# Neighbour sum: compact weight blocks for half a batch, spread by DMA into a block-diagonal buffer

## What is computed

```python
idx = _knn(x_loc, k)                          # k = 30 neighbours of each of 1024 points
...
att = jax.nn.softmax(h[..., 0], axis=-1)      # one weight per point and neighbour
xk = x.transpose(0, 2, 1)[bidx, idx]
agg = jnp.einsum('bnkc,bnk->bnc', xk, att)    # the neighbour sum
return x + agg.transpose(0, 2, 1)
```

## Time and profile before

| | before |
|---|---|
| median of three runs | 8177.31 us |
| the profiled execution's own time | 8177.04 us |
| its span, first to last instruction | 8175.2 us |
| VectorE busy over the span | 7178.0 us (88%) |
| TensorE busy over the span | 5788.3 us (71%) |
| GpSimd busy over the span | 4651.6 us (57%) |
| ScalarE busy over the span | 4377.7 us (54%) |
| granted TensorE clock, mean | 0.801 of full speed |

### The profile page before, as it was taken

How to read it: one execution, slowest core, us unless ns; L and a number is a source line. 1 busy time by engine, 2 the same in 40 slices (tenths; PEclk the granted TensorE clock), 3 DMA queues, 4 the chain that set the end, 5 groups by cost and what they waited for, 6 DMA issues and landing times. The chain is left out here.

```text
span 8175.2 us, 225464 instructions
## 1 busy us (share of the span) xinstructions
PE 5788.3 (71%) x83468; PEld 3497.5 (43%) x83468; DVE 7178.0 (88%) x9524; ACT 4377.7 (54%) x16920; POOL 4651.6 (57%) x4269
## 2 busy tenths in 40 slices
PE   7888778878877888887778778787100177777777
PEld 3444444444444444444444444444000155555555
DVE  7998988888898888989888888998498798888898
ACT  6666666666666666666666666665222322222222
POOL 5677777777777777777777777776300122222222
PEclk8888888888888888888888888887555588788888
DMA  1211112221111222211121221112300011100000
GB/s 40 70 65 65 65 65 75 74 68 66 65 65 65 75 68 74 66 65 65 65 75 65 75 67 65 65 65 75 99 0 0 14 33 33 33 28 33 32 32 28
DMA packets 245175, 459.06 MB, mean 56 GB/s; under 512 B 152636, under 2 KB 178492, under 8 KB 211260
## 3 DMA queue, kind: packets, MB, share of 16 engines
q1 hardware_dynamic: 244028, 443.74, 16.2%
HBM read 378.65 MB, written 65.01 MB: 54 GB/s over the span
## 5 line engine op out<-in xcount | busy, mean ns | idle before, releaser
L641 ACT ACTIVATE prob<-SC,row_max 128x64 f32<-128x64 f32 x6144 | 1829.8, 324 | 1733.7 <-DVE row_max L956 1599.3
L745 POOL TENSOR_TENSOR k_bd<-k_t,head_mask 128x512 f32<-128x512 f32 x1536 | 1642.0, 1090 | 30.6 <-issue 20.0
L756 POOL TENSOR_TENSOR prob<-prob,row_rec 128x512 f32<-128x512 f32 x768 | 799.5, 1041 | 1356.9 <-DVE row_rec L964 1345.5
L932 DVE MAX8 top<-dist 128x8 f32<-128x1024 f32 x1024 | 1248.1, 1219 | 126.5 <-DVE dist L934 65.0
L641 ACT ACTIVATION_READ_ACCUMULATOR prob<-SC,row_max 128x1 f32 x6144 | 1331.8, 217 | 0.0
L936 DVE FIND_INDEX8 nbr<-top,dist 128x8 uint16<-128x1024 f32 x1024 | 1247.8, 1219 | 0.3 <-issue 0.3
L549 PE MATMUL PT<-ident,prob 128*128 128x128 f32 x3072 | 600.0, 328 | 689.3 <-ACT prob_t L648 685.8
L1493 PE MATMUL DM<-placed,d_oh_a 128*128 128x32 bf16 x24576 | 675.7, 181 | 432.3 <-DVE placed L1652 382.0
L541 PE MATMUL SC<-k_bd,q_t 128*64 128x256 f32 x6144 | 955.8, 438 | 0.0
L1534 ACT ACTIVATE sph_all<-DM 128x512 f32<-128x512 f32 x512 | 305.7, 597 | 1197.6 <-PE DM L1493 1197.6
L934 DVE MATCH_REPLACE8 dist<-top,dist 128x1024 f32<-128x1024 f32 x768 | 927.5, 1208 | 0.0
(11 more groups left out here) (191 smaller groups left out, 11234.4 us busy)
## 6 DMA issues: line engine op xcount, KB each, us to landing
low_all<-low_scratch SPq DMA_DIRECT2D x256, 1024.0 KB, 4.9
ctx<-in_ctx SPq DMA_DIRECT2D x32, 512.0 KB, 4.5
mask<-in_mask SPq DMA_DIRECT2D x32, 512.0 KB, 7.3
xb<-in_x SPq DMA_DIRECT2D x32, 512.0 KB, 3.7
x_scratch<-xb SPq DMA_DIRECT2D x32, 512.0 KB, 5.1
y_scratch<-y_b SPq DMA_DIRECT2D x32, 512.0 KB, 6.6
d_x<-x_scratch SPq DMA_DIRECT2D x32, 512.0 KB, 3.8
d_y<-y_scratch SPq DMA_DIRECT2D x32, 512.0 KB, 3.3
```

Of the source, the lines that this page charges most:

```text
L641: last = act.activation(prob[:, s % 4, g * CHUNK:(g + 1) * CHUNK], SC[:, s % 2, g * CHUNK:(g + 1) * CHUNK], ACT.Exp, bias=row_max[:, s % 2 ...
L745: last = pool.tensor_tensor(k_bd[:, q % 2, ch, :].rearrange("p (h k) -> p h k", h=8), kk, hm, ALU.mult)
L756: pool.tensor_tensor(pr, pr, row_rec[:, r % 2, :].unsqueeze(2).to_broadcast([128, 8, CHUNK]), ALU.mult).then_inc(normed, 1)
L932: last = dve.max(top8[:, k, :], dist[:, tt % 2, :])
```

## The change

The matrix that TensorE reads as moving operand is block-diagonal: a partition has non-zero weights in its own quarter's 8 columns alone. The new kernel computes these 8 columns only (`compact`), for four tiles at a time (`QG` = 128 columns of groups), and four DMAs per half batch, one for each quarter of 32 partitions, copy them into their own block of `placed`. `placed` now holds half a batch in each of two slots and is set to zero once at the start. The moving operand of a matmul is then read from `placed` with a step of `QG` elements. GpSimd's parts are no longer written twice. x2, y3, y and the transposed x2 move into free space of `sph_all`, and SyncE's order of loads and stores is rewritten around the new DMAs. Unchanged names stand as before.

```diff
+QG = NT // 2 * GROUPS
-        hj2 = sb("hj2", [128, BPD, NT, GROUPS, 2], BF16)
+        hi1 = sb("hi1", [128, 2, QG], BF16)
+        iota_m = sb("iota_m", [128, 8 * QG], BF16)
-        at3 = sb("at3", [128, BPD, 3, NT, GROUPS, 2], BF16)
+        at3 = sb("at3", [128, BPD, 3, 2, QG], BF16)
-        oh_j = sb("oh_j", [128, 2, GROUPS, 32], BF16)
-        placed = sb("placed", [128, 2, 3, GROUPS, 32], BF16)
-        x2 = sb("d_x2", [128, BPD, T])
-        y3 = sb("d_y3", [128, BPD, T])
-        x2_t = sb("x2_t", [128, BPD, NT, 128])
+        oh_m = sb("oh_m", [128, 2, 8, QG], BF16)
+        compact = sb("compact", [128, 2, 3, 8, QG], BF16)
+        placed = sb("placed", [128, 2, 4, 3, 8, QG], BF16)
+        spare = [keep["sph"][:, c, 8 * HALF:8 * HALF + 4 * T].rearrange("p (w u n) -> p w u n", w=2, u=BPD) for c in (0, 2)]
+        x2, y3 = spare[0][:, 0], spare[0][:, 1]
+        x2_t, y = spare[1][:, 0].rearrange("p u (t c) -> p u t c", t=NT), spare[1][:, 1]
...
+            def spread_blocks(i, u, h):
+                b = counter(i, u)
+                sp.wait_ge(compact_ready, START + b(2, h + 1))
+                if is_first(i, u):
+                    sp.wait_ge(cleared[h], START + 1)
+                else:
+                    sp.wait_ge(dense_ready, START + b(2 * NT, NT * (h - 1)))
+                for q in range(4):
+                    sp.dma_start(placed[32 * q:32 * q + 32, h, q, :, :, :], compact[32 * q:32 * q + 32, h, :, :, :]).then_inc(placed_in[h], 16)
             def body(i, u):
                 b = counter(i, u)
+                spread_blocks(i, u, 1)
+                if not is_first(i, u):
+                    before, slot = counter(i, u - 1), (u - 1) % BPD
+                    if not is_last(i, u):
+                        sp.wait_ge(xt_ready, START + before(1, 1))
+                        sp.wait_ge(xy_ready, START + before(1, 1))
+                        sp.dma_start(x2[:, slot, :], dram["x2"][b(1, 1)]).then_inc(x2_in[slot], 16)
+                        sp.wait_ge(read_out, START + before(2, 2))
+                        sp.dma_start(y3[:, slot, :], dram["y3"][b(1, 1)]).then_inc(y3_in[slot], 16)
+                    sp.wait_ge(normed, START + before(1, 1))
+                    sp.dma_start(dram["out"][before(1)], y[:, slot, :]).then_inc(out_done[slot], 16)
+                if not is_last(i, u):
+                    spread_blocks(i, u + 1, 0)
+            spread_blocks(0, 0, 0)
             all_batches(sp, body)
...
                     pe.wait_ge(oh_ready, START + b(NT, t + 1))
-                    pe.wait_ge(placed_ready, START + b(NT, t + 1))
+                    if t % 4 == 0:
+                        pe.wait_ge(placed_in[t // 4], START + b(64, 64))
...
-                                last = pe.matmul(DM[:, x % DM_BANKS, (g % 16) * 32:(g % 16 + 1) * 32], oh_a[:, t % 2, g, :],
-                                                 placed[:, t % 2, part, g, :], start=(part == 0), stop=(part == 2))
+                                last = pe.matmul(DM[:, x % DM_BANKS, (g % 16) * 32:(g % 16 + 1) * 32].rearrange("p (q m) -> p q m", q=4),
+                                                 oh_a[:, t % 2, g, :], placed[:, t // 4, :, part, :, col], start=(part == 0), stop=(part == 2))
...
-                then(pool.tensor_copy(parts[:, 0], at_t[:, :].unsqueeze(2).to_broadcast(wide)))
+                then(pool.tensor_copy(parts[:, 0], at_t[:, :]))
...
+            pool.memset(placed[:, 1, :, :, :, :], 0.0).then_inc(cleared[1], 1)
             split_weights(counter(0, 0), 0, False)
...
-                link(dve.tensor_scalar(hj2[:, u, :, :, :].rearrange("p t g two -> p (t g) two"), hi_u[:, :].unsqueeze(2).to_broadcast(wide),
-                                       eight_q[:, 0:1], None, ALU.add))
+                link(dve.tensor_copy(hi1[:, :, :].rearrange("p h c -> p (h c)"), hi_u[:, :]))
...
-                one_hot = oh_j[:, t % 2, :, :].rearrange("p g (j two) -> p g j two", two=2)
-                dve.tensor_tensor(one_hot, hj2[:, u, t, :, :].unsqueeze(2).to_broadcast(wide),
...
-                for part in range(3):
-                    last = dve.tensor_tensor(placed[:, t % 2, part, :, :].rearrange("p g (j two) -> p g j two", two=2), one_hot,
-                                             at3[:, u, part, t, :, :].unsqueeze(2).to_broadcast(wide), ALU.mult)
+            def one_hot_blocks(b):
+                wide = [128, 2, 8, QG]
+                dve.tensor_tensor(oh_m[:, :, :, :], hi1[:, :, :].unsqueeze(2).to_broadcast(wide),
+                                  iota_m[:, :].rearrange("p (m c) -> p m c", m=8).unsqueeze(1).to_broadcast(wide), ALU.is_equal).then_inc(oh_m_ready, 1)
+            def compact_blocks(b, i, u, h):
+                if h == 0:
+                    dve.wait_ge(oh_m_ready, START + b(1, 1))
+                    dve.wait_ge(at3_ready, START + b(1, 1))
+                dve.wait_ge(placed_in[h], START + b(64))
+                wide = [128, 3, 8, QG]
+                dve.tensor_tensor(compact[:, h, :, :, :], oh_m[:, h, :, :].unsqueeze(1).to_broadcast(wide),
+                                  at3[:, u, :, h, :].unsqueeze(2).to_broadcast(wide), ALU.mult).then_inc(compact_ready, 1)
...
+                    if t == 5 and not is_last(i, u):
+                        one_hot_blocks(counter(i, u + 1))
+                    if t >= 6 and not is_last(i, u):
+                        compact_blocks(counter(i, u + 1), i, (u + 1) % BPD, t - 6)
...
+            dve.memset(placed[:, 0, :, :, :, :], 0.0).then_inc(cleared[0], 1)
             indices(counter(0, 0), 0)
             weights(counter(0, 0))
+            one_hot_blocks(counter(0, 0))
+            for h in range(2):
+                compact_blocks(counter(0, 0), 0, 0, h)
```

More of the change, by code:

```diff
@@ L1357, in neighbour_sum @@
         iota = sb("iota_a", [128, 128], BF16)
-        eight_q = sb("eight_q", [128, 1])
         minus_half = sb("d_minus_half", [128, 1])
@@ L1368, in neighbour_sum @@
         rest = sb("d_rest", [128, 2, NT * KP])
-        at3 = sb("at3", [128, BPD, 3, NT, GROUPS, 2], BF16)
+        at3 = sb("at3", [128, BPD, 3, 2, QG], BF16)
         oh_a = sb("d_oh_a", [128, 2, GROUPS, 128], BF16)
-        oh_j = sb("oh_j", [128, 2, GROUPS, 32], BF16)
-        placed = sb("placed", [128, 2, 3, GROUPS, 32], BF16)
-        x2 = sb("d_x2", [128, BPD, T])
-        y3 = sb("d_y3", [128, BPD, T])
-        x2_t = sb("x2_t", [128, BPD, NT, 128])
+        oh_m = sb("oh_m", [128, 2, 8, QG], BF16)
[4 more added lines that the diff above has]
+        x2_t, y = spare[1][:, 0].rearrange("p u (t c) -> p u t c", t=NT), spare[1][:, 1]
         dense = [keep["sph"][:, c, 0:8 * HALF].rearrange("p (m n) -> p m n", m=8) for c in (0, 2)]
-        y = sb("d_y", [128, BPD, T])
         stats = sb("d_stats", [128, 2, 6])
@@ L1393, in neighbour_sum @@
         oh_ready = sem("d_oh_ready")
-        oh_j_ready = sem("oh_j_ready")
-        placed_ready = sem("placed_ready")
+        cleared = [sem(f"cleared{h}") for h in range(2)]
+        oh_m_ready = sem("oh_m_ready")
+        compact_ready = sem("compact_ready")
+        placed_in = [sem(f"placed_in{h}") for h in range(2)]
         dense_ready = sem("dense_ready")
@@ L1410, in neighbour_sum @@
         passed = sem("d_passed")
-        CONSTS = [(ident[:, :], "ident"), (iota[:, :], "iota_a"), (eight_q[:, :], "eight_q"), (minus_half[:, :], "pow_half")]
+        CONSTS = [(ident[:, :], "ident"), (iota[:, :], "iota_a"), (iota_m[:, :], "iota_m"), (minus_half[:, :], "pow_half")]
         block = es.enter_context(nc.Block())
@@ L1443, in _ @@
                 sp.dma_start(y3[:, u, :], dram["y3"][u]).then_inc(y3_in[u], 16)
+            def spread_blocks(i, u, h):
+                b = counter(i, u)
+                sp.wait_ge(compact_ready, START + b(2, h + 1))
+                sp.sem_inc(passed, 1)
+                if is_first(i, u):
+                    sp.wait_ge(cleared[h], START + 1)
+                else:
+                    sp.wait_ge(dense_ready, START + b(2 * NT, NT * (h - 1)))
+                sp.sem_inc(passed, 1)
+                for q in range(4):
+                    sp.dma_start(placed[32 * q:32 * q + 32, h, q, :, :, :], compact[32 * q:32 * q + 32, h, :, :, :]).then_inc(placed_in[h], 16)
@@ L1445, in body @@
             def body(i, u):
                 b = counter(i, u)
[L1447 to L1453, removed]
@@ L1454, in body @@
-                sp.wait_ge(normed, START + b(1, 1))
-                sp.dma_start(dram["out"][b(1)], y[:, u, :]).then_inc(out_done[u], 16)
+                spread_blocks(i, u, 1)
[3 more added lines that the diff above has]
+                        sp.wait_ge(xt_ready, START + before(1, 1))
+                        sp.sem_inc(passed, 1)
+                        sp.wait_ge(xy_ready, START + before(1, 1))
+                        sp.sem_inc(passed, 1)
+                        sp.dma_start(x2[:, slot, :], dram["x2"][b(1, 1)]).then_inc(x2_in[slot], 16)
```

(45 more changed lines are left out.)

## The result

The changed kernel takes 8704.7 us, median of four runs (8696.9 to 8708.2), against 8177.8 us (median of four runs): 1.064 times as long (95% interval 1.0625 to 1.0661). That is 527 us slower, where 300 us faster was forecast.

The account below looks back on a forecast made before the run. VectorE, writing `placed`, was taken as the bound, with TensorE next. 8177.0 us less 31 x 9.7 (301), less 8.3 for the last batch, plus 12 at the start gave 7880 us; own range 7830 to 7930, whole range to 8100.

Parts of the forecast that it names:

- The bound before: Kernel before: VectorE is the bound, a tile's `placed` ends last; TensorE stood 26.2 us for it in two batches.
- the sum: Whole kernel: 8177.0 us less 301 for 31 batches, less 8.3 for the last batch, plus 12 at the start: 7880 us.
- I take 2.40 us: TensorE's 96 `DM` matmuls of a tile, `placed` read 256 bytes apart: 2.40 us, as before; upper end 5.28 us.
- reads at a quarter pace or worse: Rival for `DM`'s strided reads: 55 ns a matmul, 5.28 us a tile, 60.3 a batch, about 8455 us; chance 0.13.
- the loop's edge: TensorE's gap once in two batches: 1.7 us a batch, plus 0.4 for the half clock behind it.
- The non-overlapping rival: Half-pace `DM` reads that do not overlap the weight load: 38.3 ns a matmul, 49.2 us a batch, about 8100; chance 0.10.
- The late spread: DMAs into `placed` land in 14 us, 4 us behind need: 46.4 us a batch, about 8004 us; chance 0.08.
- VectorE's new products: Two products over 3072 elements on VectorE per batch, in tiles 6 and 7: 1.75 us each.
- The start: Before the first tile, 11.1 us behind XT: new memsets, first product and DMA landing add 12 us (bounds 6 and 20).
- The interval without the step: A batch from XT to XT: 35.2 + 5.1 + 1.7 + 0.4 = 42.4 us, 9.7 less than 52.1.
- `DM`'s waits: TensorE's waits in a batch for VectorE, at tiles 3, 4 and 7: together 5.1 us.
- the waits at tiles 3 and 4: TensorE waits for `oh_a` behind VectorE's moments, 2.6 us at tile 3, and behind `indices`, 1.7 us at tile 4.

Follow-up runs that it names:

- run 1: The changed kernel with each matmul reading 32 neighbouring elements of the same buffer, so other weights are summed: 7909.2 us, 0.967 of the kernel before.
- run 5: The changed kernel with a group's 8 columns innermost in `compact` and `placed`, weight parts written in pairs, three products, whole computation: 7923.5 us, 0.969 of before.
- run 6: On run 5: VectorE takes moments one tile later, the weights' transpose one earlier, indices one later; whole computation: 7824.1 us, 0.957 of before.

## Why the prediction was wrong

One step decided the sign, and it was wrong.

- **The bound before was read rightly.** VectorE's writing of `placed` ended last. Without the step, removing that work brings 269 us (run 1; 254 with the whole computation, run 5), where the sum said 297.
- **The step that failed: "I take 2.40 us" for a tile read with a 256-byte step.** The text had both ends, 2.40 and 5.28 us a tile, and took the lower. It measured 5.53. The reasoning was that 24 and 32 columns take the same 25.0 ns, so the columns do not set the pace, and that at half the clock 26.7 ns of columns hide under 29. Both rows are of contiguous reads, 3 to 4 lines a matmul, 6 to 8 ns by the price of a line found since; neither could say anything of 32 lines. Reading the price as a multiple of the array's pace was the error: it is the same at both clock levels. And the rule of the Trainium skill ("Advanced Engine Details and Errata", SBUF Cachelines) was given no weight in the sum because it gave no size, though no row of the trace bore on such a read.
- **The rival that came true** was reads at a quarter pace or worse, held at 0.13. It priced a matmul at 55 ns (57.6 measured). That this was so near is luck: the 55 ns are the pace of an fp32 column, which follows the clock, and what was met is a price of a line that does not. The time, 8455, was 250 us too low. Its interval was 60.3 us, measured 68.3. Eight tiles of 5.53 rather than 5.28 are 2.0 of it. Nearly all the rest is `AG` at the lower clock: 21.6 us busy a batch (690.5 / 32), against 14.7 at the full clock, and I counted the lower clock only behind the loop's edge.
- **The non-overlapping rival** (38.3 ns) falls: a read of 12 lines, 22.8 ns at 1.9 a line, gives a matmul of the same 25 ns as one of 4 lines. Had the read and the weight load taken turns, it would have taken longer.
- **The late spread** did not come: over the whole stage `DM` waited for these DMAs 20.3 us, all of it at the start, and in run 1, whose batches are as short as the sum had them, 20.1 us, again all at the start. They landed in 3.4 us each (median). The on-chip copies of 32 partitions are as fast as the sum had them.
- **VectorE's new products** measured 1.75 us where nothing disturbed them, as taken; the one-hot 1.18 alone (1.2 in the sum), and 1.70 in the median, beside GpSimd.
- **The start**: the first tile comes 22.2 us after XT, not 11.1, so +11.1 against +12. VectorE's memset takes 5.2 us and GpSimd's 10.3.
- **The interval without the step**: 43.8 us in run 1 (XT from 6496.06 to 7854.20), where 42.4 was worked out. `DM`'s waits fit together: (176.2 - 20) / 32 = 4.9 us, against 5.1, of which 127.0 / 32 = 4.0 are put down to the one-hot. Most of what was short is `AG`: 513.2 / 32 = 16.0 us busy a batch, against 4 x 3.68 = 14.7 at the full clock. The clock falls behind some of TensorE's other waits too, and not only at the loop's edge: behind the waits at tiles 3 and 4 an `AG` of run 1 took 4.54 us, at a mean clock of 0.80.
- The waits at tiles 3 and 4 were 2.38 and 1.39 us in a batch of run 1, where the sum had 2.6 and 1.7 (the second is 1.9 by its own terms: 1.82 + 2.28 + 0.2 - 2.4). That they come from VectorE's order is shown by run 6.

## What to carry to other kernels

Before a layout is turned so that a producer writes contiguously, look at what each reader then reads: a moving operand is charged per 16-byte line (here 1.8 to 2.0 ns each), so 32 bf16 columns should touch no more than some 12 lines to stay under the 25 ns of a small matmul (12 were hidden, 16 were not). Other types and operands over fewer partitions were not tried. A few runs of 16 bytes cost nothing, even kilobytes apart, so the inner 8 columns of a block are the ones to keep together. And where a range has ends that differ by a factor of two on the engine that becomes the bound, and nothing in the trace reads like the new form, the sign of the whole change hangs on it: the weight should lie on both ends.

## What the runs showed of the hardware that was not expected

- The price of a strided read does not follow TensorE's clock: half a tile of 48 matmuls (32 lines each) takes 2.72 us at granted clock 1.00 and 2.77 at 0.50.
- Slow reads pull the granted clock down although TensorE has almost no gap: it is 0.71 over a batch in which TensorE is busy 66.05 of 66.60 us and 0.70 over the stage, and 0.88 with the contiguous read and more waits. The fp32 matmuls beside them, unchanged, pay for it with 177 us.
- Two columns a line are not enough to hide the read: step 4 (16 or 17 lines) takes 32.6 ns at granted clock 1.00, where a contiguous matmul takes 25.
- A run of 8 that straddles a line boundary (8 lines a matmul) costs the same 25 ns as an aligned one.
